# Set-up of a two-network graph kernel: overlapping edge rows as an input, layer norm beside the searches, keys per group, node ends from a column of ones

## The chip, the cores and the metric

The kernel runs on one core of a Trainium2 chip. The metric is the device time of one execution in microseconds (us). TensorE (PE), VectorE (DVE), ScalarE (ACT) and GpSimd (POOL) work beside each other; SyncE (SP) issues plain DMAs into one queue, GpSimd issues the indirect ones (gathers by an index in SBUF).

## The reference

Two graph networks run one after the other over 6250 nodes and 200000 edges, which are sorted by their destination `dst`.

```python
h = relu(layernorm(x));  x = x + L0(h, src, dst);  h = relu(layernorm(x));  x = x + L1(h, src, dst, edge attributes)
# L0
h = h @ W_in.T + b_in
for i in range(3):
    agg = scatter_logsumexp(h[src], dst)              # per node: log of the sum of exp over its edges
    h_new = relu(layer_norm(concat(h, agg) @ W_l[i].T + b_l[i], gamma, beta))
    h = 0.5 * h + 0.5 * h_new
# L1: an MLP on each edge, a segment sum by dst, a gated update of each node
```

## The kernel before

Nodes are padded to 6272 = 49 blocks (`J`) of 128 partitions. For L0 the kernel doesn't gather the edges' features. It builds a matrix of edge counts between node blocks once, in the *count loop*, and each layer multiplies it with exp(h). The count loop goes over 49 destination blocks. For each, VectorE makes one-hot rows (`one_hots`, L1336, and `source_hots`, L1323) from the *keys* of the edges, TensorE multiplies them (`count_windows`, L689), ScalarE copies the counts out as a block (L889), and TensorE multiplies the previous block with `first_parts` (`block_sums`, L672, 49 matmuls for a block), which are the sums of the first layer; VectorE reads them (`read_sums`, L1306). Layers 1 and 2 load the blocks back from HBM. L1 then runs slot by slot over the edges, with gathers from `p_tab` (L548).

The change is in what comes ahead of the count loop, and a little behind it. Everything ahead is a chain in program order on VectorE:

1. SP loads `dst`, `src`, `firsts` (the first destination of each tile of 128 edges, copied to all partitions), `prev`, x, weights and indices, in that order.
2. VectorE packs `dst` and `src` of each edge into one integer (L1071 to L1075). SP stores it (`edge_d`, L334) and then copies it inside HBM into overlapping rows (`edge_w`, L336: 6269 rows of 128 edges, each 32 edges further than the one before).
3. VectorE searches the tile in which each of 784 windows of eight nodes begins (L1082, seven searches; the windows are 7 groups of 112). GpSimd gathers these tiles (L480), VectorE finds the edge (L1088 to L1102), which gives `gran`, the row numbers for 21 gathers from `edge_w` (L489).
4. VectorE makes two masks (L1113 to L1115), which SP stores (`drop_d`, `keep_d`, L339 to L341). Small constants follow (L1118 to L1130).
5. VectorE waits for these stores (`masks_stored`), since the layer norm of x then uses their place (L1135, L997 to L1008, reciprocal L1010). The node phase follows (L1139 to L1141): seven groups of seven blocks, turned and multiplied by `W_in` on TensorE.
6. A second search (the windows' ends: on ScalarE L829, gathers L495, L1088 again) only serves to know whether the windows fit. Then come minima and maxima of h (L1171 to L1185) and the branch by `use_counts`.
7. In `by_counts`, keys are unpacked for all groups in four operations (L1284 to L1290), turned by TensorE (L665), copied by ScalarE (L866). `make_parts` (L1295 to L1302) and `find_tiles` (L1197 to L1200) follow, and the first one-hots at L1323.

ScalarE also runs 49 searches over `firsts` (L824), which `find_tiles` turns into the tile of each node's last edge. GpSimd gathers these 49 tiles (L501), and `node_ends` (L1156 to L1166), behind the count loop, turns them into each node's last edge, its degree and `has`. It stands ahead of the last `read_sums`, and SP's loads for layer 1 wait for its `end_known`.

A chain helper, `link(...)`, makes VectorE wait for each of its own operations before the next.

Of the kernel before, what the change touches and what calls it, by code (L numbers as in the profile page):

```python
# [14 lines left out]
P = 128  # L15
# [4 lines left out]
GT = 7  # L20
# [26 lines left out]
WCOLS = WD * J  # L47
WSLOTS = 4
# [6 lines left out]
PARTS = 3  # L55
HALVES = (0, (J + 1) // 2), ((J + 1) // 2, J)
MAX_WINDOW = WE - GE + 1
# [27 lines left out]
def build(nc, x_in, dst_in, prev_in, first_in, src_in, srcl_in, attr_in, w_in, v_in, out):  # L85
    with ExitStack() as ctx:
# [12 lines left out]
        edge_d = nc.dram_tensor("edge_d", (EPAD // GE, GE), I32).ap()  # L99
        edge_w = nc.dram_tensor("edge_w", (EROWS, P), I32).ap()  # L100
# [9 lines left out]
        wrap = sb("wrap", [P, P])  # L110
        src_all = sb("src_all", [P, ET + SLOTS * TB], I32)
# [15 lines left out]
        win_last, win_tile, win_edge = (sb(n, [P, 2 * WG]) for n in ("win_last", "win_tile", "win_edge"))  # L127
        win_int = sb("win_int", [P, 2 * WG], I32)
# [30 lines left out]
        def ring(n, parts=P):  # L159
# [9 lines left out]
        dst_l, prev_l, src_l = (carve(at, ET).bitcast(I32) for at in (10272, 12320, 14368))  # L169
        drop_l, keep_l, starts, pack = carve(0, ET), carve(2048, ET), carve(4096, ET), carve(6144, ET).bitcast(I32)  # L170
        firsts = carve(8208, ET).bitcast(I32)

        NE = WG * WE
        win_edges = carve(16416, NE, WQ).bitcast(I32)
        iota_i = carve(16416 + NE, WCOLS).bitcast(I32)
        win_rows, win_end_rows = (carve(at, WG * P, WQ).bitcast(I32).rearrange("p (c e) -> p c e", c=WG)
                                  for at in (16416, 16416 + NE + WCOLS))
        win_upto = carve(0, WG * P, WQ).rearrange("p (c e) -> p c e", c=WG)
        key_a, key_b = carve(0, NE, WQ), carve(NE, NE, WQ)
# [15 lines left out]
        first_parts = carve(2 * BLK // 2, J * PARTS * D // 2).bitcast(BF16).rearrange("p (a c) -> p a c", a=J)  # L195
# [27 lines left out]
        pack_ready, pack_stored = sem("pack_ready"), sem("pack_stored")  # L223
        rows_stored = sem("rows_stored")
        edges_loaded = sem("edges_loaded")

        win_tile_known, win_fetched = sem("win_tile_known"), sem("win_fetched")
        win_end_known, win_end_fetched, win_searched = (sem(n) for n in ("win_end_known", "win_end_fetched", "win_searched"))
        gate_scaled = sem("gate_scaled")
        nodes_ready, nodes_searched, degrees_ready = sem("nodes_ready"), sem("nodes_searched"), sem("degrees_ready")  # L230
        node_tiles, starts_read, centered = sem("node_tiles"), sem("starts_read"), sem("centered")

        gran_known, gran_fetched = sem("gran_known"), sem("gran_fetched")
# [83 lines left out]
        LOADS = 5  # L317
# [3 lines left out]
        def _(sp):  # L321
            sp.sem_inc(e0.out_free, 1)
            for t, d in ((dst_l, dst_in), (src_l, srcl_in)):
                sp.dma_start(t, d.rearrange("o (p e) -> (o p) e", p=P)).then_inc(edges_loaded, DMA)
            sp.dma_start(firsts, first_in.partition_broadcast(P)).then_inc(edges_loaded, DMA)
            sp.dma_start(prev_l, prev_in.rearrange("o (p e) -> (o p) e", p=P)).then_inc(loaded, DMA)
            sp.dma_start(xres[:, :, :], x_in).then_inc(loaded, DMA)
# [49 lines left out]
            def by_counts():  # L377
# [19 lines left out]
                sp.wait_ge(end_known, 1)  # L397
# [65 lines left out]
        def _(pool):  # L463
            for t in (ident, neg_ident, shift, wrap):
                pool.memset(t[:, :], 0.0).then_inc(consts, 1)
            pool.memset(ones[:, :], 1.0).then_inc(consts, 1)
# [4 lines left out]
            pool.wait_ge(consts, 5)  # L471
# [4 lines left out]

# [8 lines left out]
            pool.wait_ge(rows_stored, DMA)  # L485
            for g in range(WG):
                for n in range(WT):
                    to = g * WE + n * P
                    pool.indirect_dma_start(win_edges[:, to:to + P], None, edge_w,  # L489
                                            bass.IndirectOffsetOnAxis(ap=gran[0:WQ, g, n:n + 1].bitcast(U32), axis=0))\  # L490
                        .then_inc(gran_fetched, DMA)

            pool.wait_ge(win_end_known, 1)
            for c in range(WG):
                pool.indirect_dma_start(win_end_rows[:, c, :], None, dst_tiles,  # L495
                                        bass.IndirectOffsetOnAxis(ap=win_int[0:WQ, WG + c:WG + c + 1].bitcast(U32), axis=0))\
                    .then_inc(win_end_fetched, DMA)

            pool.wait_ge(tile_known, 1)
            for j in range(J):  # L500
                pool.indirect_dma_start(wide[:, j, :].bitcast(I32), None, dst_tiles,  # L501
                                        bass.IndirectOffsetOnAxis(ap=end_idx[:, j:j + 1].bitcast(U32), axis=0))\
                    .then_inc(tile_fetched, DMA)
            pool.wait_ge(gran_fetched, WG * WT * DMA)
            pool.wait_ge(tile_fetched, J * DMA)

            def gather(e, c, i, table, width):
                for k in range(SLOTS):
# [996 lines left out]
```

## Time and profile before

| | us |
|---|---|
| median of 3 runs (3775.6 to 3780.91) | 3775.7 |
| profiled execution, its own time | 3775.88 |
| its span, first to last instruction | 3774.1 |
| VectorE at the first one-hot of the count loop | 282.08 |
| last sums of the first layer read | 982.76 |

Times in the rows below are microseconds from the start of the span, or durations. Set-up takes the first 282 us, the count loop ends near 969, layers 1 and 2 run to about 1570, L1 takes the rest.

### The profile page before, as it was taken

What the parts mean: (1) busy time and instruction counts of PE and PEld (TensorE: products, weight loads), DVE (VectorE), ACT (ScalarE), POOL (GpSimd) and SP (SyncE); (2) the same over time, 40 slices, a digit from 0 to 9 for tenths busy, and PEclk for the clock granted to TensorE, in tenths of its full rate; (3) what the DMA queues carried; (4) which work ended last, traced back from release to release, by engine and by line L of the source; (5) the groups of instructions that cost most, each with busy time, mean ns of one, the idle gap of its engine ahead of it and who ended that gap; (6) DMA issues with size and microseconds to landing.
All of it is one profiled execution on the core that took longest, in us unless ns stands there. A gap on an engine that the chain in (4) does not pass through costs nothing.

```text
span 3774.1 us, 59761 instructions
## 1 busy us (share of the span) xinstructions
PE 2935.2 (78%) x17152; PEld 2062.4 (55%) x17152; DVE 1652.0 (44%) x3486; ACT 1465.5 (39%) x2187; POOL 1648.5 (44%) x1721
## 2 busy tenths in 40 slices
PE   0049999999589599468888888888888888888845
PEld 0036777777489499444445545454444454555545
DVE  3159999999810500732222222222222222222227
ACT  6067888888300200123333333333333333333312
POOL 0125000000000000077777777777777777777642
PEclk9999999999799799778887887878888888888756
DMA  2103222222389298146666666666666666666510
GB/s 100 40 13 137 118 105 117 119 119 111 145 319 397 119 390 342 44 120 163 168 164 162 168 164 163 166 159 171 163 161 168 165 164 168 163 164 163 149 45 17
DMA packets 360500, 584.11 MB, mean 155 GB/s; under 512 B 42813, under 2 KB 256060, under 8 KB 341398
## 3 DMA queue, kind: packets, MB, share of 16 engines
q1 hardware_dynamic: 306038, 472.45, 37.2%
q0 software_dynamic: 54432, 111.30, 13.6%
q8 instruction: 13, 0.21, 0.0%
q14 instruction: 17, 0.14, 0.0%
HBM read 394.90 MB, written 191.89 MB: 155 GB/s over the span
## 4 chain that ended last, share of the span: by engine, by line
POOL 29%; PE 28%; issue 16%; DVE 15%; DMA 7%; SPq 3%; DVEq 2%; ACT 1%; POOLq 0%; ACTq 0%
POOL arena L548 27%; PE ps L672 13%; DVE arena L1336 6%; DMA arena<-p_tab,m_idx 6%; PE ps L747 4%; PE ps L689 4%; SPq L339 3%; PE ps L591 2%; PE ps L756 2%; PE ps L744 2%; PE ps L579 1%; POOL ends L521 1%; DVEq L1336 1%; PE ps L764 1%; DVE ends L1035 1%
## 5 line engine op out<-in xcount | busy, mean ns | idle before, releaser
L548 POOL DMA_INDIRECT arena<-p_tab,m_idx x1568 | 1486.4, 948 | 1741.2 <-issue 1708.9
L1409 DVE TENSOR_TENSOR_SCAN arena<-arena,ps 128x512 f32<-128x512 f32 x392 | 501.6, 1280 | 1037.8 <-ACT ps L934 936.8
L747 PEld LDWEIGHTS ps<-ident,arena 128*128 128x128 f32 x3136 | 480.6, 234 | 639.9 <-DMA arena<-p_tab,m_idx 482.3
L747 PE MATMUL ps<-ident,arena 128*128 128x128 f32 x3136 | 571.4, 338 | 296.8 <-DMA arena<-p_tab,m_idx 296.3
L929 ACT ACTIVATE arena<-ps 128x512 f32<-128x512 f32 x392 | 234.0, 597 | 1040.4 <-PE ps L747 1031.9
L672 PE MATMUL ps<-arena 128*128 128x192 bf16 x5635 | 494.6, 247 | 67.0 <-DVE arena L1302 66.0
L756 PE MATMUL ps<-arena,weights 128*128 128x512 f32 x784 | 530.3, 767 | 0.0
L1336 DVE TENSOR_SCALAR arena<-iota_w,arena 128x392 bf16<-128x392 f16 x2156 | 523.1, 324 | 0.0
L672 PEld LDWEIGHTS ps<-arena 128*128 128x128 f16 x5635 | 472.1, 98 | 81.0 <-issue 66.3
L689 PE MATMUL ps<-arena 128*128 128x392 bf16 x2352 | 460.9, 337 | 69.5 <-DVE arena L1336 69.0
L744 PE MATMUL ps<-arena,weights 17*128 17x512 f32 x784 | 486.1, 702 | 0.0
L689 PEld LDWEIGHTS ps<-arena 128*128 128x128 bf16 x2352 | 294.0, 145 | 197.5 <-DVE arena L1336 126.9
L764 PEld LDWEIGHTS ps<-ident,arena 128*128 128x128 f32 x1568 | 238.4, 166 | 293.8 <-issue 292.2
L889 ACT ACTIVATE arena<-ps 128x784 f16<-128x784 f32 x392 | 321.4, 820 | 72.1 <-PE ps L689 71.5
L934 ACT ACTIVATE ps<-ps,weights 128x512 f32<-128x512 f32 x392 | 259.5, 662 | 221.9 <-PE ps L756 221.8
L579 PE MATMUL ps<-ident,stage 128*128 128x128 f32 (+1 forms) x392 | 75.4, 357 | 340.2 <-DVE stage L1139 196.1
L764 PE MATMUL ps<-ident,arena 128*128 128x128 f32 x1568 | 276.8, 307 | 1.1 <-DVE arena L1409 1.1
L579 PEld LDWEIGHTS ps<-ident,stage 128*128 128x128 f32 (+1 forms) x392 | 59.5, 177 | 347.5 <-issue 344.5
L941 ACT ACTIVATE arena<-ps 128x512 f32<-128x512 f32 x392 | 231.7, 591 | 19.1 <-PE ps L764 18.8
L1306 DVE TENSOR_REDUCE ends<-ps 128x192 f32 (+1 forms) x147 | 52.7, 358 | 366.7 <-PE ps L672 366.6
L1396 DVE COPY m_idx<-src_all 128x8 int32 (+1 forms) x192 | 38.4, 200 | 386.7 <-PE ps L747 384.5
L1323 DVE TENSOR_TENSOR arena<-iota_s,arena 128x1536 bf16<-128x1536 bf16 x197 | 189.0, 959 | 0.4 <-PE ps L689 0.4
(193 smaller groups left out, 1870.6 us busy)
## 6 DMA issues: line engine op xcount, KB each, us to landing
arena<-count_d SPq DMA_DIRECT2D x66, 1568.0 KB, 8.3
arena<-keep_d SPq DMA_DIRECT2D x392, 256.0 KB, 4.4
scan_rows<-arena SPq DMA_DIRECT2D x392, 256.0 KB
count_d<-arena SPq DMA_DIRECT2D x49, 1568.0 KB
wide<-count_d SPq DMA_DIRECT2D x32, 1568.0 KB, 8.2
arena<-p_tab,m_idx POOLq DMA_INDIRECT x1568
arena<-attr_in SPq DMA_DIRECT2D x392, 34.0 KB
p_tab<-wide SPq DMA_DIRECT2D x7, 448.0 KB, 3.0
```

The costliest lines, as they stand in the source:

```text
L548: pool.indirect_dma_start(m_rows[:, k, t, :], None, p_tab, bass.IndirectOffsetOnAxis(ap=m_idx[:, k, t:t + 1].bitcast(U32), axis=0))\
L672: last = pe.matmul(ps[:, r % 2, 0:PARTS * D], blocks[r][:, a, :], rhs[:, a, :], start=(a == 0), stop=(a == J - 1), skip_group_check=True)
L689: last = pe.matmul(ps[:, 4 + s, 0:WCOLS], hot_b[q % 2][:, :, s * WT + i], hot_a[:, s, i, :], start=(i == 0), stop=(i == WT - 1))
L744: pe.matmul(x, W("W1e"), m_attr[:, k % ATTR_RING, :], start=True, stop=False, skip_group_check=True)
L747: last = pe.matmul(x[:, t * P:(t + 1) * P], m_rows[:, k, t, :], ident[:, :], start=False, stop=(t == TB - 1), skip_group_check=True)
L756: pe.matmul(m_term[k % TERM_RING], W("W2"), m_hid[:, k % HID_RING, :], start=True, stop=True).then_inc(e1.w2_done, 1)
L764: last = pe.transpose(m_back[k % 2][:, t * P:(t + 1) * P], m_scan[:, k % SCAN_RING, t * P:(t + 1) * P], ident[:, :])
L889: act.activation(blocks[r][:, :, 2 * m * WD:2 * (m + 1) * WD].rearrange("p a (w d) -> p a w d", w=2), ps[:, two:two + 2, 0:WCOLS].rearrang ...
L929: act.activation(m_hid[:, k % HID_RING, :], m_in[k % 2], ACT.Silu).then_inc(e1.silu1_done, 1)
L934: act.activation(m_term[k % TERM_RING], m_term[k % TERM_RING], ACT.Silu, bias=W("b2")).then_inc(e1.silu2_done, 1)
L1336: dve.tensor_scalar(hot_a[:, s, t, :], iota_w[:, :], keyT_a[:, t, bass.ds(w, 1)], None, ALU.is_equal)\
L1409: dve.tensor_tensor_scan(m_scan[:, k % SCAN_RING, :], m_mask[:, k, :], m_term[k % TERM_RING], before, ALU.mult, ALU.add).then_inc(e1.scan_ ...
```

## The change

- The host gives the overlapping rows as an input, `rows_in`: 6269 rows, each with 128 `dst` and 128 `src` values (1024 bytes). The packing, its store and the copy inside HBM are gone; the 21 gathers read `rows_in` and bring 256 values a row, into `wide`.
- The loads stand in another order: `firsts`, x, `dst`, `prev`, weights, vectors, indices.
- Of the seven first searches VectorE does four, ScalarE three. The search of the windows' ends is gone; the last `dst` of each gathered window answers the same question.
- The layer norm stands between the searches and the wait for the gathered tiles, with a place of its own, and reads x without a copy; the node phase stands ahead of the masks. The wait for the masks' stores moved behind the branch.
- Keys are made per group, ahead of the branch: four operations on 112x384 for each of seven groups, each group turned (TensorE) and copied (ScalarE) by itself.
- The 49 node searches on ScalarE and their 49 gathers move into the other branch, which doesn't run. `first_parts` gets a column of ones per part, so a row is 195 values (was 192) and a block's sums have the degree in column 64. Two matmuls (`upto` and `ones` with the degrees) and seven operations of VectorE (`counted_ends`) give the nodes' ends, behind `aggregate(0)`.

SyncE's queue before; `arena` is the large scratch tile:

```order
L324 DMA arena<-dst_in 128x1568
L324 DMA arena<-srcl_in 128x1568
L325 DMA arena<-first_in 128x1568
L326 DMA arena<-prev_in 128x1568
L327 DMA xres<-x_in 128x3136
L328 DMA weights<-w_in 128x963
L329 DMA rowvec<-v_in 128x1216
L330 DMA src_all<-src_in 128x1584
L334 DMA edge_d<-arena 128x1568
L336 DMA edge_w<-edge_d 6269x128
L339 DMA drop_d<-arena 128x1568
```

SyncE's queue of the change:

```order
L329 DMA arena<-first_in 128x1568
L330 DMA xres<-x_in 128x3136
L332 DMA arena<-dst_in 128x1568
L332 DMA arena<-prev_in 128x1568
L333 DMA weights<-w_in 128x963
L334 DMA rowvec<-v_in 128x1216
L335 DMA src_all<-src_in 128x1584
L340 DMA drop_d<-arena 128x1568
```

`firsts` moved from third to first, and nothing stands any more between the loads and the store of the masks.

VectorE from its searches to the row numbers, before:

```order
L1082 TENSOR_SCALAR hbuf,win_tile<-arena,win_last 128x1568 x7
L1083 TENSOR_SCALAR win_tile<-win_tile 128x7
L1084 CAST win_int<-win_tile 128x7
L1093 CAST step_f<-step_i 128x3
L1088 TENSOR_TENSOR arena<-arena,win_last 112x896
L1089 TENSOR_REDUCE win_edge<-arena 112x7
```

The same place in the change:

```order
L1061 TENSOR_SCALAR hbuf,win_tile<-arena,win_last 128x1568 x4
L1062 TENSOR_SCALAR win_tile<-win_tile 128x4
L1065 TENSOR_SCALAR win_tile<-win_tile 128x3
L1066 TENSOR_SCALAR win_tile<-win_tile 128x3
L1067 CAST win_int<-win_tile 128x7
L1071 TENSOR_REDUCE mean<-xres 128x49
L1072 TENSOR_SCALAR mean<-mean 128x49
L1073 TENSOR_TENSOR ybuf<-xres,mean 128x3136
L991 TENSOR_TENSOR arena<-ybuf 128x3136
L992 TENSOR_REDUCE var<-arena 128x49
L1075 TENSOR_SCALAR var<-var 128x49
L1081 TENSOR_TENSOR arena<-arena,win_last 112x896
```

Three searches left VectorE, and the layer norm now stands where it only waited for GpSimd's gathers.

The core of the diff:

```diff
-            for t, d in ((dst_l, dst_in), (src_l, srcl_in)):
+            sp.dma_start(firsts, first_in.partition_broadcast(P)).then_inc(firsts_loaded, DMA)
+            sp.dma_start(xres[:, :, :], x_in).then_inc(x_loaded, DMA)
+            for t, d in ((dst_l, dst_in), (prev_l, prev_in)):
                 sp.dma_start(t, d.rearrange("o (p e) -> (o p) e", p=P)).then_inc(edges_loaded, DMA)
...
-            sp.wait_ge(pack_ready, 1)
-            sp.dma_start(edge_d.rearrange("(p g) e -> p (g e)", p=P), pack).then_inc(pack_stored, DMA)
-            sp.wait_ge(pack_stored, DMA)
-            sp.dma_start(edge_w, bass.AP(edge_d.tensor, 0, [[GE, EROWS], [1, P]])).then_inc(rows_stored, DMA)
             sp.wait_ge(masks_ready, 2)
...
-                    pool.indirect_dma_start(win_edges[:, to:to + P], None, edge_w,
+                    to = 2 * (g * WE + n * P)
+                    pool.indirect_dma_start(win_edges[:, to:to + 2 * P], None, rows_in,
...
+                dve.wait_ge(gran_fetched[g // 2], min(2, WG - g // 2 * 2) * WT * DMA)
+                hi = key_hi[g % 2]
+                link(dve.tensor_scalar(hi, win_src[:, g, :, :], 7, None, ALU.logical_shift_right))
+                link(dve.scalar_tensor_tensor(key_a[:, g, :, :], win_dst[:, g, :, :], float(J), hi, ALU.mult, ALU.add))
+                link(dve.scalar_tensor_tensor(key_b[:, g, :, :], hi, -float(P), win_src[:, g, :, :], ALU.mult, ALU.add))
+                dve.tensor_scalar(key_a[:, g, :, :], key_a[:, g, :, :], win_base[0:WQ, g:g + 1], None, ALU.subtract)\
+                    .then_inc(keys_ready, 1)
...
+                dve.wait_ge(masks_stored, 6 * DMA)
+                for n in range(PARTS):
+                    dve.memset(first_parts[:, :, n * (D + 1) + D], float(n == 0)).then_inc(parts_ready, 1)
                 dve.memset(keyT_b[:, NW:NW + WSLOTS, :], 0.0)
-                dve.wait_ge(keys_copied, 4 * WT)
+                dve.wait_ge(keys_copied, 2 * WG)
                 make_parts(0, first_parts)
-                find_tiles()
...
-                node_ends()
-                read_sums(0, J - 1, 0)
+                read_first_sums(J - 1, 0)
                 aggregate(0)
+                dve.wait_ge(ends_summed, 1)
+                counted_ends()
                 layer_tail(0)
```

## Rows read from the trace of the kernel before

**Rows 1.** Windows: length; PE, PEld, DVE, ACT, POOL busy; clock, DMA share, GB/s
```profile
50.00:100.00 50.00, 0.00 (x0) 0.00 (x0) 3.73 (x11) 17.91 (x23) 0.00 (x0) 1.00 0.07 22
...
330.00:960.00 630.00, 582.52 (x4390) 456.08 (x4389) 630.00 (x2215) 510.28 (x724) 14.53 (x15) 1.00 0.28 118
```

**Rows 2.** DMA issues up to 180 us: queue, operation, count, KB, us to landing
```profile
arena<-dst_in SPq DMA_DIRECT2D x1, 784.0 KB, 4.7
...
arena<-first_in SPq DMA_DIRECT2D x1, 784.0 KB, 7.7
```

**Rows 3.** Timeline up to 54 us: start, us, engine, line; in brackets idle before
```profile
16.19 1.85 DVE L1082 TENSOR_SCALAR_CACHE_REDUCE hbuf<-arena,win_last 128x1568 f32<-128x1568 int32 x1
...
29.62 0.17 DVE L1084 CAST win_int<-win_tile 128x7 int32<-128x7 f32 x1
...
42.69 1.09 DVE L1088 TENSOR_TENSOR arena<-arena,win_last 112x896 f32<-112x896 int32 x1 [12.83 <-DMA arena<-dst_in,win_int]
...
45.97 0.18 DVE L1102 CAST gran<-gran_f 112x21 int32<-112x21 f32 x1
...
46.74 1.78 DVE L1113 TENSOR_TENSOR arena<-arena 128x1568 f32<-128x1568 int32 x1
...
50.45 119.94 SPq L339 DMA_DIRECT2D drop_d<-arena  x1
...
53.92 0.15 DVE L1130 TENSOR_SCALAR peak<-peak 128x1 f32<-128x1 f32 x1
```

**Rows 4.** Who waited for `edge_w`: us, times
```profile
  POOL arena L489: 135.7, 1
```

**Rows 5.** Timeline from 178 to 283 us
```profile
178.21 1.79 DVE L1135 COPY ybuf<-xres 128x3136 f32<-128x3136 f32 x1 [124.13 <-DMA keep_d<-arena]
...
183.86 3.42 DVE L999 TENSOR_TENSOR ybuf<-ybuf,mean 128x3136 f32<-128x3136 f32 x1
184.13 3.96 POOL L489 DMA_INDIRECT arena<-edge_w,gran  x1 [0.30 <-issue]
...
188.40 3.15 POOL L489 DMA_INDIRECT arena<-edge_w,gran  x1 [0.30 <-issue]
...
194.74 0.47 DVE L1010 RECIPROCAL rstd<-rstd 128x49 f32<-128x49 f32 x1 [0.31 <-ACT rstd L804]
195.24 1.16 DVE L1139 TENSOR_TENSOR stage<-ybuf,rstd 128x448 f32<-128x448 f32 x2
...
206.08 0.94 POOL L489 DMA_INDIRECT arena<-edge_w,gran  x1 [0.30 <-issue]
...
229.47 0.62 DVE L1141 TENSOR_TENSOR hbuf<-ps,rowvec 128x448 f32<-128x448 f32 x1 [2.36 <-PE ps L591]
...
233.57 5.52 DVE L1171 TENSOR_REDUCE extreme<-hbuf 128x64 f32<-128x3136 f32 x1
...
252.04 1.56 DVE L1284 TENSOR_SCALAR arena<-arena 112x2688 int32<-112x2688 int32 x1 [1.04 <-issue]
...
268.62 3.49 DVE L1295 TENSOR_TENSOR ybuf<-hbuf,shift_c 128x1600 f32<-128x1600 f32 x2 [8.95 <-ACT arena L866]
...
282.08 0.96 DVE L1323 TENSOR_TENSOR arena<-iota_s,arena 128x1536 bf16<-128x1536 bf16 x1
```

**Rows 6.** Timeline of VectorE in the count loop: ends of single blocks
```profile
311.38 0.35 DVE L1306 TENSOR_REDUCE ends<-ps 128x192 f32 x1
...
354.25 0.34 DVE L1306 TENSOR_REDUCE ends<-ps 128x192 f32 x1
...
409.95 0.34 DVE L1306 TENSOR_REDUCE ends<-ps 128x192 f32 x1
```

**Rows 7.** Timeline behind the count loop
```profile
968.76 4.22 PE L672 MATMUL ps<-arena 128*128 128x192 bf16 x49 [0.92 <-ACT arena L889]
...
982.04 0.21 DVE L1163 COPY start_f<-ps 128x49 f32<-128x49 f32 x1 [0.73 <-PE ps L614]
...
982.76 0.36 DVE L1306 TENSOR_REDUCE ends<-ps 128x64 f32<-128x192 f32 x1
```

More of the change, by code:

```diff
@@ L47 @@
 WCOLS = WD * J
+DVE_SEARCHES = 4
 WSLOTS = 4
@@ L528, in _ @@
             with pool.If_eq(counts, 0):
+                pool.wait_ge(tile_known, 1)
+                for j in range(J):
+                    pool.indirect_dma_start(wide[:, j, :].bitcast(I32), None, dst_tiles,
+                                            bass.IndirectOffsetOnAxis(ap=end_idx[:, j:j + 1].bitcast(U32), axis=0))\
+                        .then_inc(tile_fetched, DMA)
                 pool.wait_ge(ends_known, 1)
@@ L617, in _ @@
             node_phase(G_IN, D, [(W("w_in"), D)])
+            for g in range(WG):
+                pe.wait_ge(keys_ready, g + 1)
+                if g >= 2:
+                    pe.wait_ge(keys_copied, 2 * (g - 1))
+                for n, key in enumerate((key_a, key_b)):
+                    for i in range(WT):
+                        last = pe.transpose(ps[:, 4 + 2 * (g % 2) + n, i * WQ:(i + 1) * WQ], key[:, g, i, :], ident[0:WQ, 0:WQ])
+                last.then_inc(keys_turned, 1)
             pe.wait_ge(ext_ready, 1)
@@ L718, in by_counts @@
                 block_sums(J - 1, 0, first_parts)
-                node_starts()
+                pe.wait_ge(degrees_known, 1)
+                pe.matmul(ps[:, 2, 0:J], upto[:, :], degree[:, :], start=True, stop=True)
+                pe.matmul(ps[:, 3, 0:J], ones[:, :], degree[:, :], start=True, stop=True).then_inc(ends_summed, 1)
                 layer_product(0)
@@ L848, in by_edges, with search @@
             def by_edges():
+                def search(j):
+                    if j >= 4:
+                        act.wait_ge(nodes_searched, j - 3)
+                    act.activation(junk[:, (j % 4) * ET:(j % 4 + 1) * ET], firsts, ACT.Sign, bias=after_node[:, j:j + 1],
+                                   accum_out=sign_sum[:, j:j + 1]).then_inc(nodes_searched, 1)
+                for j in range(J):
+                    search(j)
                 with act.Fori(0, LAYERS) as l:
@@ L1079, in _ @@
+            dve.tensor_scalar(win_after[:, :], win_base[:, :], -float(WD), 0.5, ALU.mult, ALU.add).then_inc(afters_ready, 1)
+            link(dve.tensor_copy(step_f[:, :], step_i[:, :]))
+            link(dve.tensor_scalar(after_node[:, :], node_no[:, :], -1.0, -0.5, ALU.mult, ALU.add))
+            dve.wait_ge(firsts_loaded, DMA)
             junk = hbuf[:, :, :].rearrange("p j d -> p (j d)")[:, 0:ET]
[L1081 removed]
+            for c in range(DVE_SEARCHES):
                 link(dve.tensor_scalar(junk, firsts, win_last[:, c:c + 1], 0.0, ALU.is_le, ALU.add, accum_out=win_tile[:, c:c + 1]))
[L1083 removed]
@@ new lines, in _ @@
+            in_link = Chain(chain["in"])
+            dve.wait_ge(x_loaded, DMA)
+            in_link(dve.tensor_reduce(mean[:, :], xres[:, :, :], AX.X, ALU.add))
+            in_link(dve.tensor_scalar(mean[:, :], mean[:, :], 1.0 / D, None, ALU.mult))
+            in_link(dve.tensor_tensor(ybuf[:, :, :], xres[:, :, :], per_node(mean[:, :], D), ALU.subtract))
+            sum_squares(in_link, ybuf[:, :, :], first_squares)
+            dve.tensor_scalar(var[:, :], var[:, :], 1.0 / D, LN_EPS, ALU.mult, ALU.add).then_inc(var_ready, 1)
@@ new lines, in _ @@
+            in_link(dve.reciprocal(rstd[:, :], rstd[:, :]))
+            dve.wait_ge(loaded, LOADS * DMA)
+            node_phase(G_IN, lambda g, s: dve.tensor_tensor(stage[:, s, :, 0:D], group(ybuf, g),
+                                                            per_node(rstd[:, bass.ds(g * GT, GT)], D), ALU.mult),
+                       lambda g, s: dve.tensor_tensor(group(hbuf, g), product(4 + 2 * s, D), per_feature(V("b_in"), GT), ALU.add))
+            dve.sem_inc(h_ready, 1)
+            dve.wait_ge(edges_loaded, 2 * DMA)
```

248 lines of the change are left out of this document (103 added, 145 removed).

## The prediction

> **What bounds the kernel now.** I read the chain of waits over the first 400 us, then the timeline of that stretch, then windows by stage. The reader is to see three things. First, the set-up mostly waits. VectorE stands still for 124.13 us, until 178.21, for the store of the second mask [rows 5], and GpSimd for 135.7 us until `edge_w` is there [rows 4]. Both come from one transfer: the store of the first mask sits in SP's queue for 119.94 us behind the copy inside HBM [rows 3], and meanwhile the DMA share is 0.07 at 22 GB/s [rows 1]; 0.07 is about one engine of sixteen. Second, in the count loop VectorE is never idle (630.00 of 630), TensorE has 582.52, so TensorE has 47.5 us to spare, over 630 / 13.93 = 45 blocks 1.05 us in each [rows 1, 6]. Third, behind the loop TensorE has its last sums at 968.76 + 4.22 = 972.98, but VectorE reads them at 982.76, since `node_ends` stands ahead [rows 7].
>
> The Trainium skill (DMA: Bandwidth & Descriptors, "Why a DMA increments its semaphore by 16 and not by 1") says that a DMA uses the largest number of engines up to 16 that divides its slowest dimension. By that rule 6269 rows go through one engine, and the trace agrees (0.07 of the DMA time). It also says that a mask store of 128 rows uses all sixteen, which speaks against rival 2 below.
>
> **The change, step by step.** Everything that I change ahead of the loop lies on VectorE's chain, so I walk along it to the first one-hot, which stands at 282.08 now [rows 5].
>
> - *Loads.* `firsts` is first in the queue. The first load now takes 4.7 us, `firsts` as the third 7.7 (with the two ahead of it) [rows 2]. Issued at about 0.8, I take 4.7: VectorE starts at 5.6. The bound is 7.7, +3.
> - *Searches.* Seven, and one small operation, lie between 16.19 and 29.62 [rows 3]: (13.43 − 0.2) / 7 = 1.89 each. Four are 7.6; four small operations at 0.17 + 0.03 are 0.8. End: 14.0. ScalarE does its three beside it; its searches are hidden as long as they take less than 7.6 together.
> - *Tiles of the windows.* From the end of L1084 (29.79) to L1088 (42.69) are 12.9 us: seven gathers and their landing [rows 3]. The layer norm is now beside them. The rows show what that does: while VectorE runs a tensor-tensor operation of 3.42 us, a gather takes 3.96 and the next 3.15, where one by itself takes 0.94 [rows 5]. The norm has two such operations, so I add 3.0 + 2.2 = 5.2: 18.1, end 32.1. The norm itself is over sooner: without its copy, 178.21 + 1.82 = 180.03 to 195.24 is 15.2 [rows 5], so 29.2 at most. Bound below: no hold, then the norm ends last, −2.9.
> - *Row numbers.* 42.69 to 46.15 [rows 3]: 3.5. End 35.6.
> - *Reciprocal and node phase.* 0.5, then 195.24 to 230.09, 34.85 [rows 5], unchanged work. End 70.9. The 21 gathers run beside it: 21 × (0.94 + 0.30) = 26, landed by about 67.
> - *Masks and constants.* 46.74 to 54.07 is 7.3 [rows 3]. End 78.3. The stores then need no more than the loads did (4.7 to 7.7), hidden by 33 us of work; without that cover they would cost their landing.
> - *Keys.* No row has them at 112x384. An operation with one tensor costs 0.17 + 384 × (1.56 − 0.17) / 2688 = 0.37 [rows 3, 5], one with two 0.17 + 384 × (1.78 − 0.17) / 1568 = 0.56 [rows 3]. Two of each and four gaps of 0.03: 1.98 a group, 13.9 for seven. If all four ran at the slower price it would be 16.5, +2.6. Three small operations: 0.6. End 92.8. TensorE and ScalarE turn the keys behind it, one group late; they have the 11 us of the extremes to finish.
> - *Extremes to branch.* 233.57 to 252.04 [rows 5]: 18.5. End 111.3.
> - *Columns of ones.* Three tiny memsets and one more: 0.4. The unpacking, its turning and the wait of 8.95 (252.04 to 268.62) are gone.
> - *Parts.* `make_parts` runs from 268.62 to about 281.3, ahead of `find_tiles` (four operations, 0.8) and of 282.08 [rows 5]: 12.8. The first one-hot stands at 124.5. **Gain: 282.1 − 124.5 = 157.6.**
>
> *Count loop.* Three blocks took 42.87 us while GpSimd gathered the 49 tiles, four later ones 55.7, 13.93 each [rows 6]. The gathers are gone: gain 42.87 − 3 × 13.93 = 1.1; bound 0, if the first blocks were slow for another reason. Three columns more make a block's sums 3/192 of 4.22 longer, 0.07 us, inside the 1.05 to spare [rows 1, 7]: nothing. The two matmuls more run under the logarithm.
>
> *Behind the loop.* The last read moves from 982.76 to 973.1: 9.6. Seven operations of `counted_ends` at 0.21 + 0.03, as L1163 [rows 7], stand ahead of the layer's tail: 1.8. **Net gain 7.8**, with 1.5 either way, since its scan over 49 columns has no row. `has` and the degree lie under the logarithm. The loads for layer 1 come sooner, but they were waited for by nobody.
>
> Layers 1 and 2 and L1 keep their work. Sum: 157.6 + 1.1 + 7.8 = 166.5. From the profiled execution's own time, 3775.9 (span 3774.1; the median of the runs is 3775.7, 0.2 lower): **3609**.
>
> On the gathers beside the norm the Trainium skill (SBUF — State Buffer, "SBUF: two separate sides") says that a VectorE operation with two SBUF inputs takes the port pair "only against a GpSimd op that reads SBUF". Whoever counts an indirect DMA as not reading SBUF gets no hold, and the sum is 2.9 lower. The trace shows the hold (3.96 for 0.94), and I go by it.
>
> **Rivals.**
>
> 1. *TensorE becomes the bound of the count loop.* A row of `first_parts` is now 390 bytes, so every second one starts 2 bytes off a 4-byte boundary; no row shows a matmul fed like that. Up to 1.05 us a block, a quarter of 4.22, is free. If the 24 odd rows take twice the time, 24 × 0.086 − 1.05 = 1.0 more for 48 blocks, +49: 3658. **It ends slower than before** only if a block grows by 166.5 / 48 + 1.05 = 4.5, that is if all 49 matmuls take more than 2.07 times as long. At four times: 3 × 4.22 − 1.05 = 11.6, × 48 = 557, so 4166. Against it: the stationary side already reads two-byte values at a stride, and VectorE and TensorE otherwise read as before.
> 2. *The stores stall by themselves*, not behind the copy. Then 127.8 us (50.45 to 178.21) from the masks at 74.6 end at 202, where the branch wants them at 111.3: +91, 3700. Against it: the DMA share of one engine lasts the whole time [rows 1], and `edge_w` came free at the same moment [rows 4].
> 3. *The gathers of 1024 bytes are late.* The last group is wanted at 90.2; from 35.9 with 4.9 to land that allows 2.35 a gather, 2.05 without the gap, against 0.94. At twice the time nothing happens. At four times, 21 × 4.06 = 85, the keys end some 36 us later: 3645.
>
> **How the numbers follow.** Forecast 0.87, rival 1 in its mild form 0.04 and in its slower form 0.01, rival 2 0.03, rival 3 0.03; 0.02 for something that I don't see, of which half leaves nothing of the gain (0.005 same, 0.005 slower). A kernel can be told from no change here at about 0.2%, 7.5 us. Faster 0.98, same 0.005, slower 0.015. For the range: the bounds below are −2.9 and −1.5, those above +3, +2.6, +1.1, +1.5. The runs of the kernel before differ by 5.3 among themselves, which I allow on both sides, since each price is from one execution. That is 3599 to 3622; I take 3626 above, for a mild form of rival 1 or 3.
>
> **What would show it.** In the changed kernel's timeline: VectorE's fourth search done near 13.5; two of the seven tile gathers near 3 to 4 us; row numbers known at 36; node phase from 36 to 71; keys from 78 to 92, each operation 0.37 or 0.56; first one-hot at 124 to 125; blocks of the loop 13.93 apart with VectorE never idle; the last sums read right at TensorE's end. What would make me wrong is a wait for `keep_d` ahead of the memsets, VectorE idle in the loop waiting for TensorE, or a wait for `gran_fetched` ahead of a key group.

## The result and the profile after

The changed kernel takes 3615.72 us (median of 4 runs, 3614.43 to 3636.57), the kernel before 3778.3 in the same comparison (3775.6 to 3780.91). The ratio is 0.9583, with a 95% interval of [0.9547, 0.9619]. The profiled execution of the changed kernel took 3614.43, its span 3612.2.

| us from the start of the span | before | predicted | after |
|---|---|---|---|
| row numbers (`gran`) done | 46.2 | 35.6 | 32.6 |
| node phase of the set-up done | 230.1 | 70.9 | 53.9 |
| keys done, branch work begins | – | 92.8 | 77.4 |
| first one-hot | 282.1 | 124.5 | 108.9 |
| last sums of layer 0 read | 982.8 | | 799.2 |
| span | 3774.1 | | 3612.2 |

Ahead of the count loop the gain is 173.1, and I had 157.6. At the tail of layer 0 it is 182; at the end only 161.9 are left.

The first row is the load of `firsts`, from the DMA issues (queue, operation, count, KB, us to landing), against [rows 2]:

```profile
arena<-first_in SPq DMA_DIRECT2D x1, 784.0 KB, 4.4
```

The timeline of the first 65 us, against [rows 3] and the upper half of [rows 5] (start, us, engine, line; in brackets the idle time before and what ended it):

```profile
5.43 1.85 DVE L1061 TENSOR_SCALAR_CACHE_REDUCE hbuf<-arena,win_last 128x1568 f32<-128x1568 int32 x1 [1.55 <-DMA arena<-first_in]
...
13.60 0.17 DVE L1067 CAST win_int<-win_tile 128x7 int32<-128x7 f32 x1
...
17.35 3.42 DVE L1073 TENSOR_TENSOR ybuf<-xres,mean 128x3136 f32<-128x3136 f32 x1
17.98 3.60 POOL L483 DMA_INDIRECT arena<-dst_in,win_int  x1 [0.30 <-issue]
...
21.88 3.15 POOL L483 DMA_INDIRECT arena<-dst_in,win_int  x1 [0.30 <-issue]
...
29.14 1.09 DVE L1081 TENSOR_TENSOR arena<-arena,win_last 112x896 f32<-112x896 int32 x1 [1.23 <-DMA arena<-dst_in,win_int]
...
32.42 0.18 DVE L1089 CAST gran<-gran_f 112x21 int32<-112x21 f32 x1
...
33.83 3.17 PE L572 MATMUL ps<-ident,stage 128*64 128x128 f32 x14 [33.83 <-DVE stage L1095]
...
36.93 1.77 PE L584 MATMUL ps<-weights,stageT 64*128 64x64 f32 x14
...
53.24 0.62 DVE L1097 TENSOR_TENSOR hbuf<-ps,rowvec 128x448 f32<-128x448 f32 x1 [0.94 <-PE ps L584]
...
58.39 0.35 SPq L340 DMA_DIRECT2D drop_d<-arena  x1
...
62.15 0.55 DVE L1124 TENSOR_SCALAR arena<-wide 112x384 int32<-112x384 int32 x1
62.73 0.56 DVE L1125 SCALAR_TENSOR_TENSOR ends<-wide,arena 112x384 f32<-112x384 int32 x1
...
63.92 0.42 DVE L1127 TENSOR_SCALAR ends<-ends,win_base 112x384 f32<-112x384 f32 x1
```

The reader is to see that VectorE waits nowhere for long: 1.23 us for the gathered tiles, where it was 12.83, and nothing for the row gathers. Two of the seven tile gathers are held: beside VectorE's operations they take longer than the 0.93 us of one by itself, as forecast, by 3.60 + 3.15 − 2 × 0.93 = 4.9. The store of the first mask takes 0.35 in SP's queue instead of 119.94. The wait for the masks at the branch is gone too; the memset behind it starts at 95.87 with 1.25 idle before:

```profile
77.44 5.42 DVE L1153 TENSOR_REDUCE extreme<-hbuf 128x64 f32<-128x3136 f32 x1
...
95.87 0.10 DVE L1335 MEMSET arena<- 128x49 bf16 x1 [1.25 <-issue]
...
108.94 0.95 DVE L1317 TENSOR_TENSOR arena<-iota_s,arena 128x1536 bf16<-128x1536 bf16 x1
```

The count loop, against [rows 6, 7]: ends of two blocks, the block sums with their new width, and what stands behind the loop.

```profile
151.67 0.35 DVE L1285 TENSOR_REDUCE wide<-ps 128x195 f32 x1
...
165.61 0.35 DVE L1285 TENSOR_REDUCE wide<-ps 128x195 f32 x1
...
794.73 4.41 PE L665 MATMUL ps<-arena 128*128 128x195 bf16 x49 [0.92 <-ACT arena L877]
...
799.18 0.36 DVE L1285 TENSOR_REDUCE wide<-ps 128x65 f32<-128x195 f32 x1 [5.95 <-PE ps L665]
...
808.12 0.21 DVE L1292 COPY end_f<-ps 128x49 f32<-128x49 f32 x1 [0.15 <-DVE shift_c L1311]
...
809.73 0.61 DVE L1190 COPY stage<-hbuf 128x448 f32<-128x448 f32 x1
```

A block takes 165.61 − 151.67 = 13.94, from the first blocks on, and 49 matmuls of 195 columns take 4.41 (4.22 with 192). VectorE reads the last sums as soon as TensorE has them (794.73 + 4.41 = 799.14). Windows (length; PE, PEld, DVE, ACT, POOL busy; clock, DMA share, GB/s) of the set-up's node phase, of that of layer 1 and of the loop:

```profile
33.00:54.00 21.00, 19.37 (x147) 17.11 (x147) 8.37 (x14) 6.37 (x7) 15.82 (x18) 1.00 0.29 87
1076.00:1110.00 34.00, 31.02 (x147) 30.77 (x147) 20.19 (x35) 7.82 (x9) 0.00 (x0) 0.50 0.44 186
140.00:770.00 630.00, 583.59 (x4380) 466.99 (x4379) 630.00 (x2217) 515.93 (x724) 0.00 (x0) 1.00 0.28 116
```

and the same two node phases of the kernel before:

```profile
196.00:230.00 34.00, 33.36 (x147) 28.92 (x147) 7.52 (x13) 12.15 (x14) 15.10 (x16) 1.00 0.11 28
1258.00:1284.00 26.00, 19.18 (x147) 18.55 (x147) 19.62 (x35) 7.95 (x9) 0.00 (x0) 0.89 0.57 243
```

Each holds 147 matmuls. The set-up's were busy 33.36 before and are busy 19.37 now; layer 1's were busy 19.18 at a clock of 0.89 and are busy 31.02 at 0.50, the lower of the two levels (1.2 GHz). No line of the change touches the matmuls of either phase. These two swings are what my sum lacked: the first is a gain of 14, the second, which layer 2 has as well, a loss.

TensorE's rows in the set-up of the kernel before, against 33.83 and 36.93 of the timeline above:

```profile
196.07 3.16 PE L579 MATMUL ps<-ident,stage 128*64 128x128 f32 x14 [196.07 <-DVE stage L1139]
199.17 3.25 PE L591 MATMUL ps<-weights,stageT 64*128 64x64 f32 x14
```

The first 14 matmuls take the same in both kernels (3.16 and 3.17). The next 14 take 3.25 before and 1.77 in the change, and it stays so to the end of the phase: both begin at the low level, and only the changed kernel's set-up leaves it. The column for the clock says 1.00 in both windows all the same.

### The profile page after: what moved, and what is told of

It is laid out like the page before. It is cut to its first block, busy times and chain, and to the rows that moved or that the text cites. A ratio compares the mean times of both kernels' runs of the same rounds, so it can differ in the third digit from the quotient of the medians.

```text
span 3612.2 us, 59613 instructions
## 1 busy us (share of the span) xinstructions
PE 2970.1 (82%) x17152; PEld 2102.1 (58%) x17152; DVE 1628.9 (45%) x3492; ACT 1389.0 (38%) x2083; POOL 1591.1 (44%) x1667
## 4 chain that ended last, share of the span: by engine, by line
POOL 31%; PE 24%; issue 18%; DVE 17%; DMA 7%; DVEq 2%; ACT 1%; POOLq 1%; ACTq 0%; SPq 0%
POOL arena L541 29%; PE ps L665 11%; DVE arena L1330 9%; DMA arena<-p_tab,m_idx 6%; PE ps L742 4%; PE ps L584 3%; PE ps L751 2%; PE ps L739 2%; PE ps L572 1%; DVEq L1330 1%; POOL ends L509 1%; PE ps L759 1%; DVE arena L1317 1%; DVE ybuf L1202 1%; DVE ends L1023 1%
## 5 line engine op out<-in xcount | busy, mean ns | idle before, releaser
L742 PEld LDWEIGHTS ps<-ident,arena 128*128 128x128 f32 x3136 | 488.0, 237 | 623.2 <-DMA arena<-p_tab,m_idx 463.9
L742 PE MATMUL ps<-ident,arena 128*128 128x128 f32 x3136 | 579.6, 342 | 278.6 <-DMA arena<-p_tab,m_idx 278.6
L665 PE MATMUL ps<-arena 128*128 128x192 bf16 (+1 forms) x5635 | 505.6, 248 | 66.7 <-DVE arena L1275 65.8
L751 PE MATMUL ps<-arena,weights 128*128 128x512 f32 x784 | 540.5, 782 | 0.0
L665 PEld LDWEIGHTS ps<-arena 128*128 128x128 f16 x5635 | 481.8, 98 | 81.1 <-issue 66.1
L682 PE MATMUL ps<-arena 128*128 128x392 bf16 x2352 | 452.1, 336 | 70.9 <-DVE arena L1330 70.6
L759 PEld LDWEIGHTS ps<-ident,arena 128*128 128x128 f32 x1568 | 241.5, 168 | 300.7 <-issue 299.3
L759 PE MATMUL ps<-ident,arena 128*128 128x128 f32 x1568 | 278.4, 308 | 1.3 <-DVE arena L1406 1.3
L1279 DVE TENSOR_REDUCE ends<-ps 128x192 f32 (+1 forms) x98 | 35.0, 358 | 368.1 <-PE ps L665 368.1
L739 PEld LDWEIGHTS ps<-arena,weights 17*128 17x128 f32 x784 | 128.1, 204 | 80.7 <-issue 80.6
```

What stands on the lines that cost most here:

```text
L665: last = pe.matmul(ps[:, r % 2, 0:rhs.shape[2]], blocks[r][:, a, :], rhs[:, a, :], start=(a == 0), stop=(a == J - 1), skip_group_check=True)
L682: last = pe.matmul(ps[:, 4 + s, 0:WCOLS], hot_b[q % 2][:, :, s * WT + i], hot_a[:, s, i, :], start=(i == 0), stop=(i == WT - 1))
L739: pe.matmul(x, W("W1e"), m_attr[:, k % ATTR_RING, :], start=True, stop=False, skip_group_check=True)
L742: last = pe.matmul(x[:, t * P:(t + 1) * P], m_rows[:, k, t, :], ident[:, :], start=False, stop=(t == TB - 1), skip_group_check=True)
L751: pe.matmul(m_term[k % TERM_RING], W("W2"), m_hid[:, k % HID_RING, :], start=True, stop=True).then_inc(e1.w2_done, 1)
L759: last = pe.transpose(m_back[k % 2][:, t * P:(t + 1) * P], m_scan[:, k % SCAN_RING, t * P:(t + 1) * P], ident[:, :])
```

## The experiments

After the forecast two questions were open: whether the one-engine copy really was the gain, and why the node phases changed their length. Each experiment is an edit of the changed kernel, but for the first, and for two that run the changed kernel again as it is. The first four ran together, the next three on another chip, and the last three on a third.

**One part alone, on the kernel before.** The copy into `edge_w` is issued as 6256 rows (16 × 391) and 13 rows, and GpSimd waits for both; nothing else is changed.

```diff
-            sp.dma_start(edge_w, bass.AP(edge_d.tensor, 0, [[GE, EROWS], [1, P]])).then_inc(rows_stored, DMA)
+            for r0, r1 in ((0, EROWS // 16 * 16), (EROWS // 16 * 16, EROWS)):
+                sp.dma_start(edge_w[r0:r1, :], bass.AP(edge_d.tensor, r0 * GE, [[GE, r1 - r0], [1, P]])).then_inc(rows_stored, DMA)
```

> The kernel before with one edit: the copy inside HBM into overlapping rows is issued as two transfers, of 6256 and 13 rows, in place of one of 6269. Theory (the stall was one transfer on one DMA engine): 6256 is divisible by 16, the copy takes some 10 us in place of 150, the mask stores land near 58 in place of 178, and everything behind moves up by 120 us: 3778 - 120 = 3658, or 3644 if TensorE's clock in the set-up's node phase comes out high, as it did in the changed kernel (20.7 us in place of 34.9). Rival (the stores stall by themselves, or the copy is slow for its small rows whatever the engines): VectorE still waits over 100 us for the second mask, and the time stays above 3750. If the theory holds, the rest of the change (order, layer norm beside waits, fewer searches, keys, node ends) is worth 3658 or 3644 less 3616, some 30 to 40 us.

Measured: 3670.2 (3649.6 to 3674.3) against 3789.1 of before in that comparison, ratio 0.968 [0.9639, 0.9721]. Its timeline:

```profile
22.52 9.96 SPq L337 DMA_DIRECT2D edge_w<-edge_d  x2
...
47.88 0.36 SPq L340 DMA_DIRECT2D drop_d<-arena  x1
...
54.37 1.79 DVE L1136 COPY ybuf<-xres 128x3136 f32<-128x3136 f32 x1 [2.77 <-DMA keep_d<-arena]
...
159.04 0.96 DVE L1324 TENSOR_TENSOR arena<-iota_s,arena 128x1536 bf16<-128x1536 bf16 x1
```

The windows from 23 to 33 us, in which both kernels copy, first before, then with the copy split (the last two columns are the DMA share and GB/s):

```profile
23.00:33.00 10.00, 0.00 (x0) 0.00 (x0) 6.68 (x11) 10.00 (x13) 2.31 (x3) 1.00 0.08 24
23.00:33.00 10.00, 0.00 (x0) 0.00 (x0) 6.52 (x11) 10.00 (x14) 2.47 (x3) 1.00 1.00 277
```

The wait for the second mask fell from 124.13 to 2.77 us, and the first one-hot came 282.08 − 159.04 = 123.0 earlier. So one number of rows, 6269, cost some 120 us of this kernel. Of the changed kernel's 173.1 ahead of the loop 159.0 − 108.9 = 50.1 remain; 14.0 of them are TensorE's level, since the set-up's node phase took 33.4 here too, and 36.1 is the rest of the change. The run also corrected a price: its seven tile gathers lie between 29.92 and the wait's end at 40.1, 10.5 behind the row that releases them, where the kernel before needed 12.9. The copy through one engine had made the landing of the gathers longer too. And its span is only 3774.1 − 3672.5 = 101.6 shorter, 21.4 less than at the first one-hot. The node phases of layers 1 and 2, which took 31.1 and 31.0 here for 22.7, are 16.7 of that; the other 4.7 stay unexplained. What the changed kernel loses in these phases comes also to a kernel that has none of the rest of the change.

**The layer norm behind the row numbers.** The six operations of the norm (L1071 to L1075) move behind `gran`.

```diff
-            in_link(dve.tensor_reduce(mean[:, :], xres[:, :, :], AX.X, ALU.add))
...
             dve.tensor_copy(gran[0:WQ, :, :], gran_f[0:WQ, :, :]).then_inc(gran_known, 1)
+            in_link(dve.tensor_reduce(mean[:, :], xres[:, :, :], AX.X, ALU.add))
...
```

> The changed kernel with the layer norm moved behind the row numbers, where it hides nothing. Theory (the norm costs only its hold on the gathers): the tile gathers take 12.9 us with no hold (win_int to the first search of edges) in place of 15.4, the row numbers are known near 30 in place of 32.6, then the norm's 14.1 us lie on the path: the node phase starts near 45 in place of 33, +12 us. Two of the 21 row gathers are held then, with no one waiting for them. Rival (by the rule that the hold costs as much as the norm): no change within 3 us. The first one-hot should move from 108.9 to 121; if the clock of the node phase comes out low it moves by 14 more.

Measured: 3623.4 (3616.7 to 3628.0), ratio 0.9578 [0.9548, 0.9608]; the changed kernel in the same comparison 0.9558.

```profile
13.80 1.13 POOL L483 DMA_INDIRECT arena<-dst_in,win_int  x1 [10.18 <-DVE win_int L1067]
...
24.03 1.09 DVE L1072 TENSOR_TENSOR arena<-arena,win_last 112x896 f32<-112x896 int32 x1 [10.52 <-DMA arena<-dst_in,win_int]
...
27.31 0.18 DVE L1080 CAST gran<-gran_f 112x21 int32<-112x21 f32 x1
...
31.47 3.96 POOL L491 DMA_INDIRECT wide<-rows_in,gran  x1 [0.30 <-issue]
```

Without the norm beside them none of the seven gathers is held (the last is issued at 21.44 and takes 0.93), VectorE waits the whole 10.52, and the row numbers come 32.4 − 27.3 = 5.1 sooner. Now two gathers of the rows are held instead (3.96 and 3.15), and nobody waits for them. The norm hides 10.5 us of waiting for 4.9 of hold. The node phase should start 9.6 later (43.4 for 33.8, seen), but the first one-hot came 132.4 − 108.9 = 23.5 later, since the phase took 33.4 instead of 19.4:

```profile
43.00:77.00 34.00, 33.36 (x147) 28.97 (x147) 7.51 (x14) 6.38 (x7) 12.65 (x13) 1.00 0.16 47
```

This is the row of the kernel before again, 33.36 for the same 147 matmuls. Of the 23.5, 14 is TensorE's level and not the move. At the end only 2.2 us were left of them by the spans (3614.4 for 3612.2), as the phases of layers 1 and 2 were short in this execution (22.7 each, where the changed kernel's took 31.0). Against the execution of the changed kernel shown next, in which they were short too, it is 3614.4 − 3592.4 = 22.0, nearly all of the 23.5. The medians differ by 5.5.

**The changed kernel again.**

> The changed kernel, unchanged, once more, to see whether the clock levels of the node phases belong to the program or to the execution. Theory A (the level that TensorE gets in a node phase depends on small differences in timing just ahead of it): in another execution of the same program a tail of layers 1 and 2 may come out at 26 us in place of 34 of node phase, and whole times differ by steps of about 8 us (one of four runs so far was 22 above the others). Rival B (the level belongs to the program, a fixed budget that is used up sooner since set-up no longer idles): both tails come out low again, with the same 34 us, and the times agree within 3 us.

Measured: 3617.9 (3594.7 to 3620.3, 5 runs), ratio 0.9558 [0.9528, 0.9589]. The profiled execution took 3594.69. Its windows of layer 1 and layer 2:

```profile
1076.00:1110.00 34.00, 19.27 (x147) 18.64 (x147) 27.20 (x39) 9.23 (x10) 0.00 (x0) 0.80 0.44 187
1343.00:1370.00 27.00, 19.12 (x147) 18.45 (x147) 20.52 (x36) 7.95 (x9) 0.00 (x0) 0.88 0.00 1
```

The phase of layer 1 starts at 1076.6, within 0.1 us of where it started in the execution shown above, behind the same matmuls and the same idle 10.38. There it was busy 31.02, here 19.27. TensorE's rows show where the two part. First the execution of 3614.43, then this one:

```profile
1076.51 3.22 PE L572 MATMUL ps<-ident,stage 128*128 128x128 f32 x14 [10.38 <-DVE stage L1192]
1079.52 3.15 PE L584 MATMUL ps<-weights,stageT 128*128 x14
```

```profile
1076.58 3.22 PE L572 MATMUL ps<-ident,stage 128*128 128x128 f32 x14 [10.38 <-DVE stage L1192]
1079.59 2.56 PE L584 MATMUL ps<-weights,stageT 128*128 x14
...
1082.76 1.67 PE L584 MATMUL ps<-weights,stageT 128*128 x14
```

The granted clock fell in the gap ahead of the phase (0.74 from 1066 to 1076.5 in both), and both enter the phase at 0.50. In this execution it rises inside the phase (0.66 from 1080 to 1082, 1.00 from 1082 on); in the other it stays at 0.50 to the end. So the question isn't why TensorE is slow at the start of the phase, but whether it gets out of the low level. The program ahead doesn't decide that by any difference that I can see: the two executions are within 0.3 us of each other at every stage up to here, and within 0.1 at this one. Smaller differences can't be excluded. The spans differ by 3612.2 − 3592.4 = 19.8, and the two phases account for 8.2 + 8.3 = 16.5 of it.

The kernel before makes such steps as well. Its seven runs in this comparison lie at 3776.9 to 3777.4 (three) and at 3789.1 to 3802.9 (four), and the first of these groups is where its profiled execution with short phases was. Of the seven no trace is kept, so their phases weren't seen.

**TensorE busy in the gap.** I put 40 and 48 matmuls of 128x392 in 16 bits into the gap ahead of the node phases (`keep_warm`), so that TensorE doesn't idle there.

```diff
+                def keep_warm(n):
+                    for _ in range(n):
+                        pe.matmul(ps[:, 5, 0:WCOLS], iota_w[:, 0:P], iota_w[:, :], start=True, stop=True)
```

> The changed kernel with matmuls of no use (128x392, results never read) on TensorE in the gap ahead of the node phase of each layer of the first network: 40 ahead of layer 0's, 48 ahead of the other two, about 8 us of work in a gap of 10.4 us. Theory A (the level follows what TensorE did just ahead): the granted clock stays 1.00 through the gap, all three node phases run at the high level, layer tails 1 and 2 get 8 us each back, and each of the three starts 1.3 us sooner than at best: 3616 - 20 = 3596. Rival B (a budget): more work makes the granted clock lower, the tails stay at 34 us, the dummies run at the low level and take 16 us in a gap of 10.4, and the time rises by 10 to 20 us.

Measured: 3614.5 (3614.2 to 3627.0), ratio 0.9562 [0.9528, 0.9596]: no difference. Windows in the gap, and in the first and the later part of layer 1's phase:

```profile
1065.00:1075.00 10.00, 8.51 (x55) 4.98 (x52) 6.20 (x5) 2.82 (x1) 0.00 (x0) 1.00 0.81 312
1076.00:1080.00 4.00, 3.89 (x23) 3.48 (x24) 2.00 (x4) 1.83 (x2) 0.00 (x0) 0.68 1.01 430
1080.00:1106.00 26.00, 26.00 (x126) 25.98 (x125) 15.55 (x26) 5.87 (x6) 0.00 (x0) 0.50 0.40 169
```

TensorE was busy through the gap at a granted clock of 1.00, entered the phase at that level, and lost it inside the phase, which took 30.2 (31.0 without). An idle gap takes the clock, as the rows above show, but filling it doesn't keep the clock in the phase: that part of my theory falls.

**Work inside the phase.** Three such matmuls stand behind each group but the last of the three layers' node phases, alone, and with those in the gap. With them ran the changed kernel with its loads in the old order (`dst`, `prev`, `firsts`, x).

```diff
                         multiply(n0 + 2 * i + s, s, width, products, slots)
+                        keep_warm(fill)
...
-                node_phase(l * NG + G_LAYER, 2 * D, [(weights[:, bass.ds(l * D + W_COLS["w_l"][0], D)], D)])
+                node_phase(l * NG + G_LAYER, 2 * D, [(weights[:, bass.ds(l * D + W_COLS["w_l"][0], D)], D)], fill=3)
```

> The changed kernel with three matmuls of no use (128x392 of 16-bit values, results never read) behind each group of the node phases of the first network's layers; the gap ahead is left as it is. So far TensorE kept its clock through a gap filled with such matmuls and lost it a little later, inside the node phase, whose own matmuls are short and fp32. Theory A (the node phase's own work is too light to keep or win the high level, and whether it does is decided anew in each execution): with fillers the level is high in the tails of layers 1 and 2 in every execution, node phases at 23 to 24 us in place of 31, and the times gather at the lower of the two seen, 3595. Rival B (the fillers only lengthen TensorE's work): at the low level three of them take 1 us a group, the node phases go to 36 us, times near 3625.

> Both: the gap ahead of each layer's node phase filled (40, 48, 48 matmuls) and three fillers behind each group. Theory A: the granted clock is 1.00 from the sums to the end of the node phase in all three layers; the phases take 21 us in place of 22.3, 31 and 31, and every execution ends near 3592. Rival B: as with the gap alone, high through the gap and low behind it, 36 us a phase, 3625.

> The changed kernel with the loads in the old order (dst and prev ahead of the first destinations and x). Theory (the queue serves the loads one after the other, 0.8 MB in about 2 us): the searches start near 9.5 in place of 5.4, everything up to the first one-hot moves by 4 us, whole time +4. Rival (the first searches don't end last): no change at the first one-hot.

Measured: this chip takes 4392.3 for the kernel before, so only numbers of this comparison stand beside each other. Fillers 4175.3 (ratio 0.9512 [0.9481, 0.9544]), fillers and gap 4170.0 (0.9502 [0.9486, 0.9518]), old order 4178.4 (a single run). The phases of layers 1 and 2 took 24.4 and 24.9 with fillers, 21.6 and 23.9 with both, and 22.8 and 22.8 in the run of the old order, which has no fillers. The 31 us that they were to prevent didn't occur here, with or without them, so the question stayed open. In the run with both, layer 1's phase ran at a granted clock of 1.00 throughout, and layer 2's fell to 0.50 (1371 to 1375) and rose again. The order of the loads is settled, by the first search and its wait:

```profile
9.50 1.85 DVE L1061 TENSOR_SCALAR_CACHE_REDUCE hbuf<-arena,win_last 128x1568 f32<-128x1568 int32 x1 [5.62 <-DMA arena<-first_in]
```

9.50 for 5.43, and the first one-hot at 141.0, against 136.9 and 137.2 in the runs with fillers, whose set-up is the changed kernel's: `firsts` in front is worth some 4 us.

**Fillers again, two small edits, and the changed kernel beside them.** In the second kernel VectorE does three searches and ScalarE four, and two copies (`iota_w`, `iota_s`) move ahead of the first search.

```diff
-DVE_SEARCHES = 4
+DVE_SEARCHES = 3
...
+            link(dve.tensor_copy(iota_w[:, :], iota_i[:, :]))
+            link(dve.tensor_copy(iota_s[:, :, :], iota_i[:, 0:P].unsqueeze(2).to_broadcast([P, P, QUAD])))
             dve.wait_ge(firsts_loaded, DMA)
```

> The changed kernel with three matmuls of 128x392 in 16-bit behind each group of the node phases of the three layers (the same program as in the run with fillers before). Theory A (what TensorE does between the groups decides whether the phase keeps the clock): the phases of layers 1 and 2 last 22 to 25 us, not 31.0 as in the changed kernel's profiled execution; the execution is 12 to 16 us below an execution with both phases at the low level, and near 3598. Theory B (the level is a matter of the execution, not of what stands between the groups): some executions have 31 us or more, and the median stays at 3610 to 3620. It only counts where the plain changed kernel in the same call shows 31 us phases.

> The changed kernel with two edits in the set-up: VectorE does three of the seven searches and ScalarE four, and the two copies of the column numbers (iota_w, iota_s) stand ahead of the first search, where VectorE waited 1.55 us for the first load. Expected: the searches end with ScalarE's fourth, near 12.3 instead of 13.6; the copies cost about nothing where they stand now (0.2 and some 1 us) and leave the chain ahead of the keys. First one-hot near 106.5 instead of 108.9, the rest unchanged: 2 to 3 us less, below what the comparison of medians can tell. If the clock of the node phases depends on when they start, the phases at 33 us and at 1076 would show another length.

> The changed kernel itself, as a reference for the other two of this call. Expected: median 3612 to 3620, single executions from 3595 to 3620, the phases of layers 1 and 2 each near 22.8 or near 31.0 in the profiled execution.

Measured, with 4395.7 for the kernel before: fillers 4169.2 (ratio 0.9483 [0.9432, 0.9533]), small edits 4162.6 (0.9471 [0.942, 0.9523]), the changed kernel 4171.1 (0.9482 [0.9429, 0.9534]). The phases of layers 1 and 2 took 22.8 and 22.8 in the plain kernel and 24.4 and 24.9 with fillers: where the level is high anyway, the fillers cost 1.6 to 2.1 each, and what they do where it falls I couldn't test. The small edits do what they should. From their timeline:

```profile
3.91 0.36 DVE L1057 CAST iota_w<-arena 128x392 f16<-128x392 int32 x1
4.31 0.96 DVE L1058 CAST iota_s<-arena 128x1536 bf16<-128x1536 int32 x1
5.31 1.85 DVE L1063 TENSOR_SCALAR_CACHE_REDUCE hbuf<-arena,win_last 128x1568 f32<-128x1568 int32 x1
...
11.68 0.17 DVE L1067 TENSOR_SCALAR win_tile<-win_tile 128x4 f32<-128x4 f32 x1 [0.53 <-ACT ends L817]
...
12.08 0.17 DVE L1069 CAST win_int<-win_tile 128x7 int32<-128x7 f32 x1
```

The copies fill the wait for `firsts` exactly (no idle is left at 5.31), the searches end at 12.25 for 13.66 in the plain kernel here, and the first one-hot comes at 134.2 for 136.9, 2.7 sooner. The medians can't tell 2.7 us; by its one trace it is the better kernel, and the best version that I ran.

## Why the prediction was right, and where its steps were off

3609 was forecast, with 3599 to 3626; it came to 3615.7. The kernel's gain is the one that I named. The total is as close as it is by luck in part: misses of both signs met. The execution with short phases in layers 1 and 2 took 3594.69, which is below my range, and one of the four runs of the result, 3636.57, is above it.

- *The stores behind the copy: right.* Undoing the copy's bad row count alone gave 123.0 at the first one-hot. Rival 2, stores that stall by themselves, is dead: the same stores, behind a copy of 9.96 us, took 0.36 in the queue and 2.77 of waiting.
- *Loads and searches: right.* 5.43 for 5.6, and 13.8 for 14.0; ScalarE's three searches were hidden.
- *Tile gathers beside the norm: the hold right, the landing too long.* I had 12.9 + 5.2 = 18.1; it is 15.4. The hold is 4.9, measured also by taking the norm away. The 12.9 was read from rows in which the one-engine copy ran beside the gathers; without it they need 10.5. The miss is 2.7, and with 0.2 from the searches the row numbers are 3.0 early. Here the step that failed is a price read in a stretch that the change itself was to clear.
- *The node phase: the term that was mis-sized.* I carried 34.85 from the kernel before, which with the reciprocal's step made 70.9 − 35.6 = 35.3; it took 53.9 − 32.6 = 21.3, 14.0 less. The work is the same 147 matmuls, 33.36 busy before and 19.37 after; TensorE got out of the low level behind the first 14 of them, which it hadn't before. The timeline gave it away: 14 matmuls of the one line took 3.25 in it, and the very same kind takes 1.77 in the changed kernel, though the column for the clock says 1.00 in both windows. I took the column's word, and had not asked what the phase costs at the other level.
- *Masks, constants and keys: 1.7 dearer.* Masks and constants took 8.3 for 7.4, the keys 15.3 for 14.5. The shift and the two combined operations took 0.55 to 0.56, my dearer price, and the subtraction 0.42, between my two.
- *Branch, ones, `make_parts`: right.* 18.4 for 18.5, and 13.1 for 13.2 together.
- So 157.6 + 3.0 + 14.0 − 1.7 + 0.2 = 173.1, as measured.
- *Count loop and behind it: right.* From the first one-hot to the layer's tail 709.6 became 700.8, a gain of 8.8; I had 1.1 + 7.8 = 8.9. The seven operations took 1.6 for 1.8. Rival 1 is dead: 49 matmuls took 4.41 for 4.22, and VectorE was busy 630.00 of 630. Three columns more alone would make 4.29, so 0.12 us a block is left over; whether the rows that start 2 bytes off cost it, no run shows. It lies inside the 1.05 to spare and costs the kernel nothing.
- *Rival 3: dead.* No key group waited for its gathers.
- *"Layers 1 and 2 and L1 keep their work. Sum": the step that failed.* They kept their work, but not their time. The gain was 181.9 where the node phase of layer 1 starts, 173.6 where it ends, 164.4 at the end of that of layer 2, and 161.9 at the end. Each node phase took 31.0 for 22.7, at 0.50 for 0.89. So 20 us went back, 16.6 of them in these two phases. It isn't a fixed price of the change: the changed kernel has an execution without it (span 3592.4, which is 3774.1 − 181.7, all of the gain), and the kernel before seems to have it at times. Whether the change makes it more frequent is open: on the quicker chips one of the changed kernel's nine runs is near 3595, and seven of the eleven of the kernel before are under 3781. Of the 14 won and the 16.6 to 20 lost, neither was in my range's reasons; that it held owes much to their opposite signs.

What decides whether a phase leaves the low level stays open. Shown is that an idle gap brings TensorE to it, that filling the gap alone didn't keep it off in the one trace that has this on the quicker chips, and that one program, with stages that start within 0.3 us of each other, went both ways. In each of the twelve traces the phases of layers 1 and 2 are both long (30 to 31) or both short (under 25). In the set-up the phase took 19.2 to 19.4 in the three traces from the quicker chips in which it began near 34 us, and 33.4 where it began at 43, 72 or 196; I have no experiment that moves it with all else fixed, so this is an observation and no cause.

## What to carry to other kernels

Look first for a stretch in which everything waits and the DMA share stands at one engine's worth; here it was one copy with a row count that 16 doesn't divide, and splitting it into 6256 and 13 rows gives some two thirds of the whole gain in three lines. Then, before carrying a duration over from the trace, ask what ran beside it and at which clock: the gathers' 12.9 contained the neighbour that the change removes, and TensorE's 33.4 was the low level of a phase that takes 19.4 once TensorE leaves it. Where a chain runs through small fp32 matmuls, give its term two prices, and read the level from the duration of one matmul, since the column for the clock can read 1.00 over matmuls that take 0.23 us where others take 0.13.

## What the runs showed of the hardware that I had not expected

- The same program, in step to 0.3 us, ran the node phases of its last two layers at 31.0 us each in one execution (3614.4) and at 22.8 in another (3594.7). Both entered them at a granted clock of 0.50; in one it never rose.
- 48 matmuls in 16 bits kept the clock at 1.00 up to the phase, and the fp32 phase lost it all the same (0.68, then 0.50).
- Seven gathers land 10.5 us behind their release where the one-engine copy is absent or split, and took 12.9 beside it (DMA share 0.08 from 23 to 33 us).
- On two of the chips the kernel before takes 4392 to 4396 us where the others take 3778 to 3789, and the changed kernel 4171 for 3616. There its set-up has a hole, some 20 us long in all six traces of these chips. This row is from the changed kernel run beside the small edits; VectorE waits 19.91 us in the middle of the node phase, which ends at 82 instead of 54, and the first one-hot comes at 136.9 for 108.9:

```profile
62.35 0.62 DVE L1097 TENSOR_TENSOR hbuf<-ps,rowvec 128x448 f32 x1 [19.91 <-remote]
```

The profile names no instruction of this core as the releaser. The message stage of L1 is longer there as well (its gathers run from 1459 to 3950 instead of 1448 to 3411). I can't say why from these traces. The saving there was 4395.7 − 4171.1 = 224.6, more than the 162.6 here.
